# A graph layer whose nodes are laid out in rows of 49 per partition ahead of the loop

## What is computed

```python
hl = x @ Wl.T + bl                       # one table row per node
hr = x @ Wr.T + br
s = (take(hl, src) + take(hr, dst)) * alpha          # alpha: one row per edge
s = where(s >= 0, s, 0.2 * s)
e = exp(s - take(segment_max(s, dst), dst))
att = e / take(segment_sum(e, dst), dst)
out = layernorm(x + segment_sum(take(x, src) * att, dst))
```

## Time and profile before

| | us |
|---|---|
| median of 3 runs | 1168.29 (1168.25 to 1172.6) |
| the profiled execution | 1168.55 |
| its span | 1166.5 |
| busy in the span: PE / DVE / ACT / POOL | 1083.9 / 1081.4 / 950.3 / 853.4 |

### The profile page before, as it was taken

The page is one execution under the profiler, slowest core; times in us unless marked ns, Lnnn a source line. Parts: engine busy times, 40 slices in busy tenths (PEclk is TensorE's granted clock), DMA queues, the critical chain, the costliest instruction groups (busy, mean ns, idle before and its releaser), DMA issues.

```text
span 1166.5 us, 35708 instructions
## 1 busy us (share of the span) xinstructions
PE 1083.9 (93%) x9359; PEld 903.1 (77%) x9359; DVE 1081.4 (93%) x1466; ACT 950.3 (81%) x2396; POOL 853.4 (73%) x879
## 2 busy tenths in 40 slices
PE   5779999999999999999999999999999999999885
PEld 5648888888788878787887888787877878878763
DVE  6549999999999999999999999999999999999988
ACT  2548888888888888888888888888888888888895
POOL 6477777777777777777777777777777777777772
PEclk9889999999999999999999999999999999999998
DMA  8676666666666666666766666666666666666623
GB/s 221 226 218 194 187 187 189 182 193 189 180 187 185 187 183 187 185 185 186 187 184 181 186 186 184 184 186 178 187 181 183 186 188 184 184 187 185 173 64 110
DMA packets 220971, 213.49 MB, mean 183 GB/s; under 512 B 32765, under 2 KB 193796, under 8 KB 220682
## 3 DMA queue, kind: packets, MB, share of 16 engines
q0 software_dynamic: 40320, 109.96, 33.9%
q1 hardware_dynamic: 180005, 100.86, 31.2%
q10 hardware_dynamic: 461, 0.40, 0.1%
HBM read 200.39 MB, written 11.47 MB: 182 GB/s over the span
## 4 chain that ended last, share of the span: by engine, by line
POOL 55%; issue 19%; PE 15%; DVE 4%; DMA 3%; ACT 2%; SPq 1%; ACTq 0%; DVEq 0%; POOLq 0%
POOL xg L389 54%; PE ps_w L580 5%; PE ps_u L545 3%; PE ps_u L549 2%; PE ps_sT L538 2%; PE ps_z L567 1%; DVE acc L891 1%; DVE stats L962 1%; PE ps_q L561 1%; PE ps_q L589 1%; POOL attr L372 1%; DMA acc<-x_in 1%; DMA attr<-chunk_rows,chunk_at 1%; DMA line<-step_lines 1%; SPq L269 1%
## 5 line engine op out<-in xcount | busy, mean ns | idle before, releaser
L389 POOL DMA_INDIRECT xg<-gather_rows,srcT x832 | 798.8, 960 | 266.8 <-issue 252.1
L580 PE MATMUL ps_w<-onehot,ex 128*128 128x128 f32 x3328 | 407.5, 276 | 3.6 <-ACT acc L708 2.5
L580 PEld LDWEIGHTS ps_w<-onehot,ex 128*128 128x128 f32 x3328 | 389.6, 193 | 4.3 <-issue 4.3
L901 DVE TENSOR_TENSOR_SCAN ps_F<-line,B,ps_sT 128x512 f32<-128x512 bf16 x208 | 266.0, 1279 | 2.0 <-DMA line<-step_lines 1.0
L549 PEld LDWEIGHTS ps_u<-right,onehotT 128*128 128x128 bf16 x2496 | 161.8, 98 | 122.5 <-issue 120.5
L912 DVE TENSOR_TENSOR_SCAN B<-line,ps_F 128x512 f32<-128x512 bf16 x208 | 251.1, 1207 | 0.0
L545 PE MATMUL ps_u<-xg,ident 128*128 128x512 f32 x416 | 219.7, 610 | 26.8 <-DMA xg<-gather_rows,srcT 21.6
L672 ACT ACTIVATE onehotT<-ps_q,ones 128x512 bf16<-128x512 f32 x208 | 142.9, 687 | 67.0 <-PE ps_q L561 46.5
L549 PE MATMUL ps_u<-right,onehotT 128*128 x2496 | 178.2, 220 | 0.0
L925 DVE TENSOR_TENSOR ex<-ps_z,xg 128x512 f32<-128x512 f32 x208 | 142.7, 686 | 32.3 <-ACT ps_z L688 30.3
L705 ACT ACTIVATE acc<-ps_w 128x768 f32 x208 | 170.4, 819 | 0.2
(11 more groups left out here) (183 smaller groups left out, 883.7 us busy)
## 6 DMA issues: line engine op xcount, KB each, us to landing
attr<-edge_attr_in SPq DMA_DIRECT2D x832, 64.0 KB
line<-step_lines SPq DMA_DIRECT2D x208, 128.0 KB
xg<-gather_rows,srcT POOLq DMA_INDIRECT x832
gather_rows<-acc SPq DMA_DIRECT2D x12, 512.0 KB, 8.4
edge<-step_lines SPq DMA_DIRECT2D x202, 4.0 KB
acc<-x_in SPq DMA_DIRECT2D x6, 448.0 KB, 6.6
xg<-x_in SPq DMA_DIRECT2D x6, 448.0 KB, 3.8
out<-attr SPq DMA_DIRECT2D x6, 448.0 KB, 3.0
```

The source lines that it names most:

```text
L389: pool.indirect_dma_start(out=xg[:, k % SLOTS, i, :], out_offset=None, in_=rows_dram, in_offset=bass.IndirectOffsetOnAxis(ap=srcT[:, k * W ...
L580: last = nc.tensor.matmul(columns, ex[:, (k - 1) % 2, c, i, :], onehot[:, (k - 1) % 3, i, :], start=(i == 0), stop=(i == WIDE - 1), skip_g ...
L901: V.tensor_tensor_scan(ps_F[:, :], line[:, k % LINES, 0:GE], ps_sT[:, :], B[:, (k - 1) % 3, GE - 1:GE], ALU.add, ALU.max).then_inc(F_ok, 1)
```

## The change

In front of the loop partition p (0 to 126) holds the 49 nodes from p * 49 on, so that 127 x 49 = 6223 nodes (FULL = 127) lie in 127 partitions, and the last 27 (TAIL) in partition 127. A block b is then node p * 49 + b of every partition. The seven loads of x take 7 rows that follow each other in DRAM for each of 127 partitions, the stores of table rows 4; two small transfers of their own (x_tail, tail_out) carry the 27. VectorE zeroes the unused places of partition 127 at its start (x_zero), in place of GpSimd's memset of the last block. The transposed copy xT_all keeps the order of nodes, since the products with Wr and the loop need it: by_lane is a view of it with a step of 49 nodes, through which ScalarE writes and TensorE reads the left factor. SP's wait for p_in moves from ahead of the second chunk to ahead of the third.

```diff
+    FULL = N // BLOCKS
+    TAIL = N - FULL * BLOCKS
...
+        by_lane = xT_all.rearrange("f b n -> f (b n)").rearrange("f (p b) -> f b p", b=BLOCKS)
...
+            nodes = x[0:FULL * BLOCKS, :].rearrange("(p b) d -> p b d", b=BLOCKS)
             for c in range(CH):
-                b0, b1 = c * CH, min((c + 1) * CH, BLOCKS - 1)
-                if c == 1:
+                b0, b1 = c * CH, (c + 1) * CH
+                if c == 2:
                     sp.wait_ge(p_in, 80)
-                if c == CH - 1:
-                    sp.wait_ge(c_set, 1)
-                    sp.dma_start(x_all[0:ROWS_LAST, BLOCKS - 1, :], x[(BLOCKS - 1) * P:N, :])\
-                        .then_inc(x_in[c], 16)
-                sp.dma_start(x_all[:, b0:b1, :],
-                             x[b0 * P:b1 * P, :].rearrange("(b p) d -> p b d", p=P)).then_inc(x_in[c], 16)
+                if c == 0:
+                    sp.dma_start(x_all[FULL:P, 0:TAIL, :], x[FULL * BLOCKS:N, :].rearrange("(a b) d -> a b d", a=1)).then_inc(x_tail, 16)
+                if c == TAIL // CH:
+                    sp.wait_ge(x_zero, 1)
+                sp.dma_start(x_all[0:FULL, b0:b1, :], nodes[:, b0:b1, :]).then_inc(x_in[c], 16)
...
-            last128 = (BLOCKS - 1) * P
+            rows = rows_dram[0:FULL * BLOCKS, :].rearrange("(p b) c -> p b c", b=BLOCKS)
             for q in range(QUADS):
                 sp.wait_ge(left_ok, q + 1)
-                b0, b1 = q * QUAD, min((q + 1) * QUAD, BLOCKS - 1)
-                if q == QUADS - 1:
-                    sp.dma_start(rows_dram[last128:N, :], table[0:ROWS_LAST, BLOCKS - 1, :]).then_inc(rows_out[q], 16)
-                else:
-                    sp.dma_start(rows_dram[b0 * P:b1 * P, :].rearrange("(b p) c -> p b c", p=P),
-                                 table[:, b0:b1, :]).then_inc(rows_out[q], 16)
+                b0, b1 = q * QUAD, min((q + 1) * QUAD, BLOCKS)
+                sp.dma_start(rows[:, b0:b1, :], table[0:FULL, b0:b1, :]).then_inc(rows_out[q], 16)
+                if b0 < TAIL <= b1:
+                    sp.dma_start(rows_dram[FULL * BLOCKS:N, :].rearrange("(a b) c -> a b c", a=1), table[FULL:P, 0:TAIL, :])\
+                        .then_inc(tail_out, 16)
...
-            nc.gpsimd.memset(x_all[:, BLOCKS - 1, :], 0.0).then_inc(c_set, 1)
...
             pool.wait_ge(src_sb, 2)
+            pool.wait_ge(tail_out, 16)
...
-                pe.wait_ge(x_in[c], 16 + 16 * (c == CH - 1))
+                pe.wait_ge(x_zero, 1)
+                pe.wait_ge(x_tail, 16)
+                pe.wait_ge(x_in[c], 16)
...
-                    last = nc.tensor.matmul(ps_left[q % 2][:, i * D:(i + 1) * D], xT_all[:, q * QUAD + i, :],
+                    last = nc.tensor.matmul(ps_left[q % 2][:, i * D:(i + 1) * D], by_lane[:, q * QUAD + i, :],
...
-                nc.scalar.activation(xT_all[:, q * QUAD:q * QUAD + n, :],
+                nc.scalar.activation(by_lane[:, q * QUAD:q * QUAD + n, :],
...
             V = nc.vector
+            V.memset(x_all[P - 32:P, TAIL:BLOCKS, :], 0.0).then_inc(x_zero, 1)
```

## The result

The changed kernel takes 1524.94 us (median of 4 runs, 1523.12 to 1526.83) against 1169.51 us: the ratio is 1.3031, 95% interval 1.3005 to 1.3058. It is 355 us slower.

A forecast was written before the change was run, and what follows sets the result against it. GpSimd's gathers pace the kernel, starting once table rows land. On one engine, 3 + 174 (x) + 250 (rows) + 7 + 1.5 us puts the first gather at 435.5, 387 later: 1168.3 + 387 = 1555 us, range 1500 to 1600.

The forecast's parts named there:

- The mechanism: Before the first gather: 127-partition loads and stores share one engine in SP's queue, 387 us later; one engine's chance 0.89.
- The two-engine rival: 127-partition transfers fall to two engines: first gather at 223.5 us, 1343 us in all; chance 0.04, with another few.
- the share of 0.06: Sign in the changed kernel: from about 10 us, long stretches with DMA share near 0.06, until about 430 us.
- equal shares: Transfers use the largest number of engines up to 16 that divides both slowest dimensions; 127 is prime, so one.
- Two terms of the sum: On the one engine before the first gather: x packets 174 us, table rows 250 us.
- the engine's sixteenth of the other traffic: Before the first gather, the lone engine also carries a sixteenth of 2.35 MB: 7 us.
- The 22.5 GB/s of two lone engines: Earlier trace's speed, used for table rows if stored in 1 KB pieces: 280 us, the upper bound.
- SP issues all seven loads up front: At the start, SP issues the x loads at once; stores queue before loads finish, so the engine never runs dry.
- The rival on the other side: All 16 engines take part; first gather waits for srcT at 44.34 us, 1164 us in all; chance 0.07.
- whatever moves 48.73 moves the whole kernel one for one: The end is the first gather's start, 48.73 us, plus 1117.8 us, so its shifts reach the end in full.
- The steps of 49: Strided by_lane copies and left products before the loop: from nothing to doubling L425; covered while stores take 20 us.
- the bound from above: Strided left products: doubling L425, 1.06 us of each quad's 1.33, adds 14 us over thirteen quads.

The follow-up runs named there:

- 125 on five: Changed kernel with x loads cut into 112 and 15 partitions and table-row stores into 125 and 2: 1206.94 us.
- a cut at 127: Kernel before, old layout, with its twelve table-row stores cut into 127 partitions and 1: 1410.92 us.
- only x on one engine: Changed kernel with only the table-row stores cut into 112 and 15 partitions, x loads left at 127: 1303.15 us.
- The idea at its best: Changed kernel, x in 112 and 15 partitions, stores of all 128 into a longer table, no tail_out: 1171.11 us, 1.0004 of the kernel before.
- the kernel with 128 partitions and steps: Changed kernel, x cut 112 and 15, 128-partition stores into a longer table, no tail_out, transposed x still in steps of 49: 1171.11 us.
- the kernel with both cuts: Changed kernel with x loads and table-row stores both cut into 112 and 15 partitions: 1174.95 us, 1.0011 of the kernel before.

## Why the prediction was right

**The mechanism held step by step.** 127 partitions went over one engine, for loads and for stores; loads and stores used the same one, in SP's order; packets were 512 B for x and 4 KB for rows; the first gather waited for the rows, and its delay came out at the end nearly one for one (355.4 us there, 357.4 between the profiled spans, 355.4 between the medians). The two-engine rival fell with the share of 0.06, and equal shares were confirmed by 125 on five. That one engine is the whole cause is shown, not argued: the cuts at 112 take the loss away, and a cut at 127 brings it into the old layout.

**Two terms of the sum were too large.** x, with the first 3 us and the engine's sixteenth of the other traffic, was put at 3 + 174 + 7 = 184 us and was through at 160.5: 512 B took 23.4 ns (889 packets in 20.8 us) on the lone engine, not the 28 that each of sixteen busy engines needed in the earlier trace rows. So the packets of x were 6223 x 23.4 ns = 146 us for 174; the other traffic took what is left, some 12 us by this difference for the 7, and made up for a little of it. The rows were put at 250 us and took 242, 155 ns a packet for 160. Together 31 us: 435.5 predicted, 404.1 measured. The 22.5 GB/s of two lone engines in the earlier trace rows would have been the nearer row for x as well, had I not kept it for 1 KB pieces.

**What was wrong without harm here.** "SP issues all seven loads up front": each issue lasted some 20 us, and with them the chunk transfers behind them were late (GpSimd's wait for chunk_at is 63.4 us instead of 9.1). It stayed hidden behind the rows. Even with only x on one engine, where that wait is 64.4 us, srcT was there at 172.8 us and the first gather waited for the rows until 182.8:

```profile
172.24 0.58 DVE L857 CAST srcT<-ps_F 128x416 int32<-128x416 f32 x1
```

**The rival on the other side was priced too well.** Sixteen engines were to give 1164 us (48.73 - 44.34 is 4.4 us and not the 4.3 that stood there, which changes nothing), since "whatever moves 48.73 moves the whole kernel one for one". Here that held for the delay and not for the gain. The experiments brought the first gather to 46.9 and 45.1 us, and the last one moved by 0.8 and 0.6 us, because the wait for the step tables comes next. The steps of 49, for which I left everything between nothing and double, cost 0.86 us a quad, 11 us over thirteen, where the bound from above was 14. The idea at its best, in a kernel that computes the whole layer, comes out at 1.0004, no difference from the kernel before.

## What to carry to other kernels

Before a transfer from SP takes a number of partitions other than 128, factor that number: in these runs SP's queue cut a transfer into equal shares, as many as the largest divisor up to 16, and 127 partitions in place of 128 cost 238 us on the old layout. Keep the full 128, if need be by making the target longer; a cut at 112 brings back all the engines, but not all of their speed. When an edit makes the last condition of a wait come earlier, look up the next wait on that engine too before counting the gain.

## What the runs showed of the hardware

- SP's queue spreads a transfer over 1, 2, 5 and 16 engines for outer sizes of 127, 106, 125 and 128; GpSimd's spreads 127 over 16.
- A lone engine moves 22 GB/s in 512 B packets (loads of x), 24 in 1 KB and 26 in 4 KB (stores of table rows); one of sixteen busy ones about 17.7, 23.6 and 25.2 (283, 378 and 403 GB/s by 16, with some other traffic among it).
- Stores cut in 112 and 16 partitions move 297 GB/s where 128 at once move 378, with all engines busy in both (share 0.97 and 1.07). What differs is seven partitions an engine instead of eight, and also a second, small transfer for each quad; which of the two slows them wasn't tested.
- An issue on SP lasted 19.68 us, as long as one transfer of 127 packets on the lone engine; the stores' issue takes 0.32 us (median) in the kernel with 128 partitions and steps.
- A step of 49 elements makes ScalarE's write of 512 columns 1.08 us instead of 0.60, and TensorE's f32 weight load from there 313 ns instead of 192 (the kernel with both cuts against the kernel before; without the step 0.60 us and 192 ns again). VectorE's write with a step of 8 had not foretold it.
